# A fused attention and gated feed-forward block: one-row key mask, fp16 row maxima, weight casts on ACT, squares for the range check spread over later turns

## What is computed

```python
Q = _split_heads(query, H) * depth ** (-0.5)          # query = layernorm(x)
logits = jnp.einsum('bhqd,bhkd->bhqk', Q, K) + b[0]
logits = logits + -1e+30 * (1.0 - mask)
weights = jax.nn.softmax(logits, axis=-1)
out = jnp.einsum('bhqk,bhkd->bhqd', weights, V)
...
gate = jnp.einsum('bsd,hd->bsh', x, wg)               # weights are int32 * 1/127, hidden size 768
up = jnp.einsum('bsd,hd->bsh', x, wu)
h = jax.nn.silu(gate) * up
return jnp.einsum('bsh,dh->bsd', h, wd)
...
x = x + jnp.tanh(g_xattn[0]) * attention(ctx, layernorm(x), mask, b)
x = x + jnp.tanh(g_ffn[0]) * ffn(layernorm(x), w_gate, w_up, w_down)
```

## Time and profile before

| | |
|---|---|
| median of 3 runs | 163.39 us (163.21 to 163.62) |
| profiled execution, device time | 163.07 us |
| its span, first to last instruction | 161.3 us |
| busy: PE, DVE, ACT, POOL | 139.9, 122.9, 102.8, 91.1 us |
| mean granted clock of PE | 0.996 |

### The profile page before, as it was taken

The page is one execution under the profiler, slowest core; times in us unless marked ns, Lnnn a source line. Parts: engine busy times, 40 slices in busy tenths (PEclk is TensorE's granted clock), DMA queues, the critical chain, the costliest instruction groups (busy, mean ns, idle before and its releaser), DMA issues.

```text
span 161.3 us, 4203 instructions
## 1 busy us (share of the span) xinstructions
PE 139.9 (87%) x1459; PEld 106.6 (66%) x1459; DVE 122.9 (76%) x348; ACT 102.8 (64%) x215; POOL 91.1 (56%) x139
## 2 busy tenths in 40 slices
PE   0768689958796999999999999999999998899970
PEld 0245557735476787968796879687877857676850
DVE  4887899999997878997899689557944856775731
ACT  4327689967556786767675777666767645466530
POOL 6343360542854694689465946644675578784530
PEclk9999999999999999999999999999999999999998
DMA  4699900000000000010002000100020010010022
GB/s 111 195 358 380 326 4 0 6 0 0 0 4 0 6 0 0 6 65 0 4 0 69 2 0 4 65 6 0 0 69 0 0 65 6 0 65 4 0 71 73
DMA packets 7257, 7.92 MB, mean 49 GB/s; under 512 B 816, under 2 KB 6464, under 8 KB 7232
## 3 DMA queue, kind: packets, MB, share of 16 engines
q1 hardware_dynamic: 7056, 7.34, 13.7%
q10 hardware_dynamic: 176, 0.27, 0.6%
HBM read 5.51 MB, written 2.10 MB: 47 GB/s over the span
## 4 chain that ended last, share of the span: by engine, by line
PE 65%; DVE 21%; issue 6%; POOL 2%; DMA 2%; ACT 2%; POOLq 0%; DVEq 0%; ACTq 0%
PE ps L1305 21%; PE ps L1327 10%; PE ps L1123 4%; PE ps L1237 4%; DVE neg_max L991 4%; PE ps L1243 4%; PE ps L1214 3%; PE ps L1216 3%; PE ps L1184 3%; PE ps L1187 3%; PE ps L1257 3%; PE ps L1277 2%; DVE stats L883 2%; DVE gated L1040 2%; DMA x_sb<-in_x_dram 2%
## 5 line engine op out<-in xcount | busy, mean ns | idle before, releaser
L1305 PE MATMUL ps<-n_t,w_gu_t 128*128 128x256 f16 x384 | 49.9, 273 | 1.1 <-DVE h L1051 0.9
L1305 PEld LDWEIGHTS ps<-n_t,w_gu_t 128*128 128x128 f16 x384 | 36.2, 98 | 10.7 <-ACT n_t L786 2.5
L667 POOL TENSOR_TENSOR h<-h 128x256 f16<-128x256 f32 x48 | 32.2, 672 | 16.8 <-ACT h L804 16.2
L795 ACT ACTIVATE tanh_h<-ps 128x256 f32<-128x256 f32 x48 | 18.4, 384 | 17.4 <-PE ps L1305 17.3
L1327 PE MATMUL ps<-w_d_t,h 128*128 128x256 f16 x192 | 28.3, 272 | 0.8 <-DVE x_sb L862 0.4
L991 DVE TENSOR_REDUCE neg_max<-ps 128x4 f32<-128x512 f32 x32 | 21.5, 686 | 8.3 <-PE ps L1187 7.9
L1040 DVE SCALAR_TENSOR_TENSOR gated<-tanh_h,ps 128x256 f32<-128x256 f32 x48 | 19.8, 412 | 6.7 <-ACT tanh_h L795 6.7
L621 POOL TENSOR_TENSOR rstd<-var_eps,neg_half 128x2 f32<-128x2 f32 x16 | 11.1, 697 | 21.8 <-DVE var_eps L890 21.7
L804 ACT ACTIVATE h<-h 128x256 f16<-128x256 f32 x48 | 20.0, 417 | 5.2 <-DVE h L1051 5.1
L748 ACT ACTIVATE probs<-ps,key_bias 128x512 f32<-128x512 f32 x32 | 22.0, 686 | 0.4 <-PE ps L1216 0.4
L1051 DVE SCALAR_TENSOR_TENSOR h<-ps,gated 128x256 f32<-128x256 f32 x48 | 20.4, 424 | 1.7
(11 more groups left out here) (97 smaller groups left out, 221.9 us busy)
## 6 DMA issues: line engine op xcount, KB each, us to landing
x_sb<-in_x_dram SPq DMA_DIRECT2D x8, 256.0 KB, 8.6
out_dram<-x_sb SPq DMA_DIRECT2D x8, 256.0 KB, 2.1
kv<-in_ctx_dram SPq DMA_DIRECT2D x3, 256.0 KB, 8.3
w_raw<-in_L_ffn_w_gate_dram SPq DMA_DIRECT2D x1, 768.0 KB, 6.8
w_raw<-in_L_ffn_w_up_dram SPq DMA_DIRECT2D x1, 768.0 KB, 8.5
w_raw<-in_L_ffn_w_down_dram SPq DMA_DIRECT2D x1, 768.0 KB, 8.4
kv<-in_ctx_dram ACTq DMA_DIRECT2D x1, 256.0 KB, 3.9
mask_raw<-in_mask_BxS_ik_dram ACTq DMA_DIRECT2D x1, 8.0 KB, 2.3
```

Of the source, the lines that this page charges most:

```text
L667: pool.tensor_tensor(h16[:, r % 2, m, 1, :], h32[:, n % NHB, :], h16[:, r % 2, m, 0, :], ALU.subtract).then_inc(h_low, 1)
L1305: ins = pe.matmul(dst, lhs, rhs, start=(w == 0 and (k, l) == terms[0]), stop=(k, l) == terms[-1], skip_group_check=True)
```

## The change

**Mask.** The mask of the last chunk is also loaded as one row (`mask_row`), and one DVE instruction makes a one-row bf16 bias from it (`bias_row`: 0 or -42496). The bias matmul of the row maxima contracts over one row in place of 128. The exponential's bias is made for the last chunk alone (`exp_bias`). `mask_parts` and `mask_rows` move to the wide path. The mask's transposition comes after the first queries.

**Maxima.** DVE writes the row maxima as fp16 into the tile that is transposed; `max_split` is gone from the narrow path. The limit for keys goes from 60000 to 7500.

**Weights.** `w_cast` is an ACT instruction; the odd ones of `w_t` are evicted by ACT.

**Check.** The squares stand in every third entry of `chores` from turn 3 on, the last one, the comparison and the sum of the flag in the last three entries of turn 7.

**Start.** The low parts of the first keys are made by DVE (`k_rest`). The DMAs of the second x piece and second key piece are issued ahead of those of the gates; on ACT's queue the keys come second and the full mask third.

```diff
@@ -54,7 +54,8 @@
 H_SHRINK = 1.0 / 8.0
 SQUARES = 512
 WARM_UP = 8
-K_LIMIT = 60000.0
+K_LIMIT = 7500.0
+SHUT_OUT = -42496.0
 
 
 
@@ -119,7 +120,7 @@
     if kind == "q_stack":
         return "dve" if step[1:] == (1, 1) else "act"
     if kind == "w_t":
-        return "dve"
+        return "act" if step[1] % 2 else "dve"
     if kind == "w_wide":
         return "act" if step[1] % 2 else "dve"
     return None
@@ -140,16 +141,16 @@
     queries = lambda h: [("q_stack", h // 2, 2 * (h % 2) + i) for i in range(2)]
     maxima = lambda h: [("row_max", h // 2, c, 2 * (h % 2) + i, g) for i in range(2) for g in range(NG)]
     sq = lambda i: ("squares", i)
-    steps = [("stats", 1, 0), ("mask_t",), ("warm_up",), ("norm1", 0), ("high", 1, 0), ("low", 1, 0), ("k_parts", 0),
-             ("mask_parts",), ("mask_rows",), ("dup", 0), ("stats", 1, 1), ("q_stack", 0, 0), ("k_stack", 0),
-             ("norm1", 1), ("q_stack", 0, 1), ("high", 1, 1), ("low", 1, 1), *maxima(0)[:3], ("dup", 1),
-             *maxima(0)[3:], sq(0), ("q_stack", 0, 2), ("max_split", 0), ("max_t", 0), ("q_stack", 0, 3),
-             ("k_parts", 1), ("stats", 1, 2)]
-
-    chores = [[sq(1)], [("w_cast", 0)], [sq(2), sq(3)], [("k_stack", 1)], [("w_t", 0), sq(4)],
-              [("w_cast", 1), ("w_t", 1), sq(5)],
-              [sq(6), sq(9)], [("w_t", 2)], [sq(7), ("w_t", 3)], [sq(8), ("check",)], [("flag_sum",), ("y_scale",)], [("w_cast", 2)],
-              [("w_t", 4)], [("w_t", 5)], [], [("k_parts", 2)], [("k_stack", 2)]]
+    steps = [("bias_row",), ("stats", 1, 0), ("warm_up",), ("k_parts", 0), ("norm1", 0), ("k_rest", 0),
+             ("high", 1, 0), ("low", 1, 0), ("mask_cast",), ("dup", 0), ("k_stack", 0), ("stats", 1, 1),
+             ("q_stack", 0, 0), ("q_stack", 0, 1), ("mask_t",), ("norm1", 1), ("high", 1, 1), ("low", 1, 1),
+             *maxima(0)[:2], ("exp_bias",), maxima(0)[2], ("dup", 1), *maxima(0)[3:], ("q_stack", 0, 2),
+             ("max_t", 0), ("q_stack", 0, 3), ("k_parts", 1), ("stats", 1, 2)]
+
+    chores = [[], [("w_cast", 0)], [], [("k_stack", 1)], [("w_t", 0)], [("w_cast", 1), ("w_t", 1)],
+              [], [("w_t", 2)], [("w_t", 3)], [], [("y_scale",)], [("w_cast", 2)],
+              [("w_t", 4)], [("w_t", 5)], [], [("k_parts", 2)], [("k_stack", 2)]] + [[]]
+    chores += [part for i in range(9) for part in ([sq(i)], [], [])] + [[sq(9)], [("check",)], [("flag_sum",)]]
     units = [(h, m) for h in range(R) for m in range(MT)]
     LAG = 3
 
@@ -535,10 +542,10 @@
         @block.sync
         def _(sp):
             load_x(sp, 0)
+            load_x(sp, 1)
+            load_kv(sp, 1)
             for n, g in enumerate((g_xattn, g_ffn, attn_b)):
                 sp.dma_start(gates[:, n:n + 1], g.partition_broadcast(P)).then_inc(gates_loaded, 16)
-            load_x(sp, 1)
-            load_kv(sp, 1)
             load_x(sp, 2)
             for i, w in ((0, w_gate), (1, w_up)):
@@ -677,10 +684,11 @@
 
         @block.scalar
         def _(act):
+            act.dma_start(mask_row[:, :, :], mask[:, LAST * P:SK].unsqueeze(0)).then_inc(mask_row_loaded, 16)
+            load_kv(act, 0)
             act.dma_start(mask_raw[:, :], mask.rearrange("b (c k) -> (b c) k", k=P)).then_inc(mask_loaded, 16)
-            load_kv(act, 0)
             act.wait_ge(pool_done, CONSTS)
-            act.activation(max_sel[:, :, :], head_rows[:, :].unsqueeze(2).to_broadcast((P, NH, P)), ACT.Copy
+            act.activation(max_sel16[:, :, :], head_rows[:, :].unsqueeze(2).to_broadcast((P, NH, P)), ACT.Copy
                            ).then_inc(selector_ready, 1)
 
                         act.wait_ge(work_filled, plan.filled(step))
                         dst, src = wide_weights_out(step)
                         act.activation(dst, src, ACT.Copy).then_inc(emptied_by["act"], 1)
+                    elif kind == "w_cast":
+
+                        i = step[1]
+                        act.wait_ge(w_loaded[i], 16)
+                        act.activation(w16[:, i, :], w_raw[:, i, :], ACT.Copy).then_inc(w_cast, 1)
+                    elif kind == "w_t" and emptied_by_engine(kind, step) == "act":
+                        act.wait_ge(work_filled, plan.filled(step))
+                        act.activation(*weights_out(step), ACT.Copy).then_inc(emptied_by["act"], 1)
                     elif kind == "squares":
 
@@ -825,22 +849,31 @@
 
             def mask_steps(step):
 
-                dve.wait_ge(mask_loaded, 16)
-                dve.tensor_copy(mask_f[:, :], mask_raw[:, :]).then_inc(mask_cast, 1)
                 dve.wait_ge(work_filled, plan.filled(step))
                 dve.tensor_copy(mask_k[:, :], bank32(plan.bank(step))[:, 0:B * NC]).then_inc(emptied_by["dve"], 1)
                 dve.wait_ge(*plan.emptied(step))
+                mine(dve.tensor_scalar(exp_bias[:, :], last_mask, -1.0, 1.0, ALU.mult, ALU.add))
+                mine(dve.tensor_scalar(checks[:, 0:B * NC], mask_k[:, :], 0.0, None, ALU.not_equal))
+                mine(dve.tensor_scalar(checks[:, NZERO:NZERO + B], last_mask, 1.0, None, ALU.is_ge))
+                wait_mine()
+
+                mine(dve.scalar_tensor_tensor(
+                    out=checks[:, 0:B * NC].rearrange("p (b c) -> p b c", c=NC)[:, :, LAST], in0=last_mask, scalar=0.0,
+                    in1=last_mask, op0=ALU.not_equal, op1=ALU.not_equal))
+
+            def exp_bias_steps():
+
+                dve.wait_ge(gates_loaded, 48)
+                mine(dve.tensor_scalar(exp_bias[:, :], exp_bias[:, :], MASK_STEP, gates[:, 2:3], ALU.mult, ALU.add))
+                wait_mine()
+
+                dve.tensor_scalar(exp_bias[:, :], exp_bias[:, :], gates[:, 2:3], 0.0, ALU.subtract, ALU.min
+                                  ).then_inc(exp_bias_ready, 1)
+
+            def mask_parts_steps():
+
                 mine(dve.tensor_scalar(key_bias[:, :], mask_k[:, :], -1.0, 1.0, ALU.mult, ALU.add))
-                mine(dve.tensor_scalar(checks[:, 0:B * NC], mask_k[:, :], 0.0, None, ALU.not_equal))
-                last = mask_k[:, :].rearrange("p (b c) -> p b c", c=NC)[:, :, LAST]
-                mine(dve.tensor_scalar(checks[:, NZERO:NZERO + B], last, 1.0, None, ALU.is_ge))
                 wait_mine()
-                mine(dve.memset(checks[:, 0:B * NC].rearrange("p (b c) -> p b c", c=NC)[:, :, LAST], 0.0))
+                        dve.tensor_scalar(bias_row[:, :, :], mask_row[:, :, :], -SHUT_OUT, SHUT_OUT, ALU.mult, ALU.add
+                                          ).then_inc(bias_row_ready, 1)
+                    elif kind == "mask_cast":
+                        dve.wait_ge(mask_loaded, 16)
+                        dve.tensor_copy(mask_f[:, :], mask_raw[:, :]).then_inc(mask_cast, 1)
                     elif kind == "mask_t":
                         mask_steps(step)
+                    elif kind == "exp_bias":
...
+                        b = step[1]
+                        dve.wait_ge(k_high, b + 1)
+                        full, high, low = key_parts(b)
+                        dve.tensor_tensor(low, full, high, ALU.subtract).then_inc(k_low, 1)
                     elif kind == "k_parts":
 
                         b = step[1]
@@ -922,12 +971,6 @@
                         if b >= 2:
                             dve.wait_ge(work_filled, plan.filled(("k_stack", b - 2)))
                         dve.tensor_scalar(high, full, K_LIMIT, -K_LIMIT, ALU.min, ALU.max).then_inc(k_high, 1)
-                    elif kind == "w_cast":
-
-                        i = step[1]
-                        dve.wait_ge(w_loaded[i], 16)
-                        dve.tensor_scalar(w16[:, i, :], w_raw[:, i, :], W_LIMIT, -W_LIMIT, ALU.min, ALU.max
-                                          ).then_inc(w_cast, 1)
                     elif kind == "check":
                         dve.wait_ge(squares_summed, NSUMS)
                         dve.tensor_scalar(checks[:, B * NC:NZERO], square_sums[:, :], W_LIMIT * W_LIMIT, None,
                         else:
-                            dst = neg_max[:, qt, g * HG:(g + 1) * HG]
+                            if first and h == 0:
+                                dve.wait_ge(zeros_written, 1)
+                            if first and h >= 2:
+                                dve.wait_ge(work_filled, plan.filled(("max_t", h - 2)))
+
+                            dst = max_cols16[:, qt, g * HG:(g + 1) * HG]
                         dve.tensor_reduce(dst, bank32(plan.bank(step)).rearrange("p (h k) -> p h k", h=HG),
                                           AX.X, ALU.max, negate=not is_wide).then_inc(emptied_by["dve"], 1)
@@ -1183,22 +1228,33 @@
                                 h = g * HG + j
                                 pe.matmul(bank32(n)[:, j * P:(j + 1) * P], q_stacks[:, b, h, qt * P:(qt + 1) * P],
                                           k_stacks[:, b, h, :], start=(j == 0), stop=False, skip_group_check=True)
```

(13 more changed lines are left out.)

83 lines of the change are left out of this document (50 added, 33 removed).

## The result

The changed kernel takes 170.83 us (median of 4 runs, 168.18 to 174.63), the kernel before 163.31 beside it: ratio 1.033, 95% interval 1.027 to 1.039, slower. The forecast was 160.6, with a range up to 162.7. The profiled execution took 169.26 us, its span is 167.4 (161.3 before).

The account below looks back on a forecast made before the run. PE, busy throughout 51.2 to 125 us, was taken as the bound there, chains at both ends. Start and turns 0 to 2 give -3.8, turn 7 +1.0, sum -2.8 us: 160.3 profiled, 160.6 median, range 159.0 to 162.7.

Parts of the forecast that it names:

- The one-row bias matmul I cost at nothing: Row maxima on PE: length goes with columns, so no change; bounds 0 and a gain of 7 us.
- Rival (b): Turn 0: after a 2 us gap PE's clock rises only after turn 0, 4.9 us more, 165.5; chance 0.08.
- The start: Before the first scores: a shorter chain brings them at 17.2 in place of 18.99, a gain of 1.8 us.
- at nothing, and at 0.5 us as an upper end: Start: cost of the DMAs, with second x and key pieces beside the keys, which must be there at 4.8.
- Turns 0 to 2: Turns 0 to 2: less DVE work and no flag wait; start and turns together give 3.8 us.
- Cast 2 then ends at 35.25 and PE transposes at 35.35: Turn 2: ACT's third weight cast lets PE transpose at 35.35, not 37.94, -2.6 us.
- The full stage: Turns 3 to 6: PE has no gap, so 3.8 us carry through; the squares on ACT cost nothing.
- Turn 7: Turn 7: comparison and flag instructions in DVE's queue cost 1.0 us, between 0.7 and 1.9, all reaching the end.
- rule on the shared port: Turn 7: flag instructions on DVE each exposed to POOL's; by that rule alone the sum would be -2.0 us.
- Rival (a): ACT's queue is the new bound: slow casts, late first keys and the flag give 162.9; chance 0.2.
- Rival (c): One contraction row is cheaper, or the clock rises before 9 us: 0.4 to 3 us more gain; chance 0.07.
- (d): Gain lost before turn 3 because x, keys or a bank wait hold turn 2: 163.4, no change; chance 0.05.

Follow-up runs that it names:

- bias128: The changed kernel with the bias matmul again over 128 contraction rows, 127 of them zero: 163.95 us, ratio 1.006 to the kernel before.
- before_k64: The kernel before with only its bias matmul cut to the first 64 rows: 167.53 us, ratio 1.027.
- a_fill: The changed kernel with eight matmuls over ones filling PE's gap ahead of 16.58 us: 170.30 us, ratio 1.038 to the kernel before.
- b_start: bias128 with the start's DMAs in the order of before and the one-row bias made later: 162.47 us, ratio 0.999 to the kernel before.
- all3: bias128 with the old DMA order, eight matmuls filling the gap and the flag in turn 6: 162.37 us, ratio 0.998 to the kernel before.
- cast2_dve: all3 with the third weight cast moved from ACT to DVE: 161.64 us, ratio 0.992 to the kernel before.
- wt_late: all3 with the two last weight transposes one chore later, the cast left on ACT: 161.48 us, ratio 0.989 to the kernel before.
- casts_dve: all3 with all three weight casts and all weight evictions on DVE: 160.55 us, ratio 0.984 to the kernel before.
- before_k3x2: before_k3 with a second bias matmul over 3 rows of zeros directly ahead of the first: 177.22 us, only its trace used.
- before_k3: The kernel before with only its bias matmul cut to the first 3 rows: 168.13 us, ratio 1.022.

## Why the prediction was wrong

**The step that failed** is "The one-row bias matmul I cost at nothing". Its bounds reached from 0 to a gain of 7 us. The text took the matmul's length, 379 ns for 512 columns, as its price, and no bound was put on the side of a loss, although no row had one contraction row. The length was right (385 ns, median of 32). The price isn't a length but the distance between starts, and that grew from 0.44 to 0.64 us per group. The result is +2.46 us in the stretch where PE has no gap, shown in both directions (bias128, before_k64) and equal to 0.03 us, and 0.9 us from the end of turn 0 on. When it is undone the ratio goes from 1.033 to 1.006, 4.4 us; that holds 3.3 us of the clock too, less what bias128's later keys cost it. The Trainium skill's sentence on changes of the tiling mode might have warned; the prediction didn't weigh it, and the page doesn't say that few rows alone are another mode.

In the profiled executions the change came out 8.9 us behind the forecast (+6.1 for -2.8). By the stretches, rounded: the one row 3.4 (2.46 and 0.9), the low clock of turn 0 3.3, the start 1.9, the rest of turns 0 to 2 0.8, and turn 7 cost 0.4 less than forecast. The low clock had no term in the sum; it stood among the rivals alone.

**Rival (b), the clock**, was seen and underpriced. Its mechanism came true at its place: the gap was 2.07 us (2 us forecast), and the clock rose only at 28 us, later than the 20 us named. Its price (4.9 us) came to 3.3, with an upper bound of 4.0 by a_fill. It differed in one thing: the clock had been up since 8.43 and fell, it wasn't late. The rival's chance was 0.08. The prediction read the transposes of the earlier trace rows as what lifted the clock. In b_start 24 transposes, the last 16 of them at 9.98, run at half speed (1.89 us for 16), and the clock rises at about 15, behind row-maximum matmuls. That agrees with the Trainium skill, TensorE: Matmul & The Clock Gate, "PE-mode transpose". The kernel before still reads the other way: its clock was up at 13.44, and since the warm-up ended at 8.8 PE had done nothing but transposes. In the changed kernel the transposes at 8.43 were fast at once, directly behind the warm-up. So what lifted it is open.

**The start** gave nothing (+0.09) where 1.8 us were forecast. The DMAs, "at nothing, and at 0.5 us as an upper end", failed: the keys were 1.6 us late in the changed kernel, the norm at 6.95 and not 5.65, the queries at 10.10 and not 8.9. With the old order (b_start) the first scores are still at 18.84 and not 17.2. There x came late (its statistics at 4.61, 3.53 before), so the norm was at 6.78 and the queries at 9.98; the second norm came at 12.77, 0.4 us earlier than before and not 1.5; and `exp_bias` put 0.73 and 0.23 us of small DVE instructions ahead of the third maximum, the first one beside a POOL instruction. The forecast hadn't counted those at that length. The clip, the low part (0.69, forecast 0.65) and ACT's eviction were as forecast.

**Turns 0 to 2** were given 2.0 us beyond the start. With the row and the start mended (b_start) they gave 1.2. No wait for the check is left in turn 1, and the casts took 1.48 us (forecast 1.45), both right. "Cast 2 then ends at 35.25 and PE transposes at 35.35" failed: counted from the first scores the forecast is 18.1 us, b_start has 18.6 and all3 as well, but PE stood there for 1.83 us. The forecast took the total for ACT as unchanged and so the place as good; cast2_dve and wt_late show 0.7 to 0.9 us in the place of that cast, casts_dve 1.8 for all three casts and the evictions.

**The full stage** had no gap, and the squares are hidden in it: bias128 and before both take 76.42 us. **Turn 7**: the flag cost 1.0 by forecast, 0.57 in the changed kernel and 0.74 in bias128. Its five instructions took 0.14 to 0.16 us each:

```profile
132.40 0.16 DVE L976 TENSOR_SCALAR checks<-square_sums 128x10 f32<-128x10 f32 x1
133.31 0.16 DVE L986 TENSOR_REDUCE verdict<-ps 1x1 f32<-1x26 f32 x1
133.83 0.14 DVE L994 TENSOR_SCALAR wide_flag<-verdict 1x1 int32<-1x1 f32 x1
136.02 0.60 PE L1384 MATMUL ps<-w_d_t,h 128*128 128x256 f16 x4 [0.80 <-DVE x_sb L895]
```

The wait of the earlier trace rows went from 0.39 to 0.80. The prediction's rule on the shared port cost nothing there: the instruction at 132.40 ran beside one of POOL (131.78 to 132.51), the two at 133.31 and 133.40 beside another (133.01 to 133.68), and none was longer for it. It shows at 8.37 in b_start: a cast of 16 by 128 took 1.17 us beside a POOL instruction from 8.26 to 9.46, and 0.21 in the changed kernel, where it stood ahead of it.

**Rival (a)**, ACT's queue, is a part of what happened (the 1.83 us), with an end far from its 162.9. Rival (c) had the one row cheaper and was the opposite of what came; (d), no gain before turn 3, didn't hold once row and start were mended (b_start is 1.3 us ahead at turn 2's transposes). The upper ends of the forecast's own terms add to 162.8 (163.4 - 1.3 - 1.2 + 1.9), not to the 162.0 of the text. The forecast's own figure, 160.6, was reached by casts_dve, without the one row and without ACT's casts; that is luck, not a confirmation.

## What to carry to other kernels

Before a matmul gets fewer rows or weight columns than its neighbours, look at the starts around a place where the kernel already changes between them: here 0.1 us per change was nothing once and 2.5 us in 16 groups of a PE that has no gap, and padding the rows with zeros to 128 cost nothing. Bound an operation that no row shows on the side of a loss as well, and price instructions of PE by the distance between starts. When work moves to another engine, choose its place there by when its result is needed; that the engine's total allows it says nothing about the place. And issue the transfer that the chain waits for ahead of any small one.

## What the runs showed that was not expected

- A matmul over 3 or 64 contraction rows between full ones costs 0.2 us more than one over 96 or 128, and two in a row cost it once.
- The longest stretches at 1.2 GHz behind the first scores stand in kernels with that matmul: until 28 us in the changed kernel, until about 33 in before_k3x2, against 21.9 in b_start, 22.9 in bias128 and none in the kernel before. But before_k64 has none either and before_k3 only until 19.9. Whether such a matmul keeps the clock down is open.
- The granted clock reads 1.00 in windows where lengths say 1.2 GHz before the first rise (a_fill at 17.50: 0.42 us per 512 columns; at full clock it is 0.21).
- The cast of 1536 int32 elements took 0.95 us on DVE as a clip before and 0.94 as a plain copy in casts_dve (at 26.20), where POOL was idle. Beside POOL instructions the same copy took 1.53 (at 34.73) and 1.64 us (at 22.04). ACT took 1.48 at any place.
- The issue of a 2 KB load of one partition took 1.19 to 1.25 us on ACT's queue, that of the keys' 256 KB 0.36 to 0.45.
